# Second attention: where the tensor engine issues a group's first logits, two groups ahead

## The reference, cut to what matters

```python
std_logits = jnp.einsum('bhqd,bhkd->bhqk', q, k) * scale
incidence = jnp.einsum('bqhp,bkhp->bhqk', read_lines, J_write)
weights = decays[:, None, None] ** diffs_pos[None] * past[None].astype(x.dtype)
bias = incidence * weights[None] * bias_scale[None, :, None, None]
logits = jnp.where(causal_mask[None, None], -jnp.inf, std_logits + bias)
attn = jax.nn.softmax(logits, axis=-1)
out = jnp.einsum('bhqk,bhkd->bqhd', attn, v).reshape(B, T, D)
return out @ w_out.T + b_out
```

## Time and profile before

| | us |
|---|---|
| median of 3 runs | 1814.32 |
| lowest, highest | 1808.61, 1819.41 |
| span of the profiled execution, first to last instruction | 1776.1 |
| median of the runs less that span (start and end of the program, not in the profile) | 38.2 |
| busy in the span: tensor, vector, scalar, GpSimd | 1455.7, 1274.7, 935.2, 694.1 |
| mean granted clock of the tensor engine | 0.912 |

### The profile page before, as it was taken

How to read it: one execution, slowest core, us unless ns; L and a number is a source line. 1 busy time by engine, 2 the same in 40 slices (tenths; PEclk the granted TensorE clock), 3 DMA queues, 4 the chain that set the end, 5 groups by cost and what they waited for, 6 DMA issues and landing times. The chain is left out here.

```text
span 1776.1 us, 37567 instructions
## 1 busy us (share of the span) xinstructions
PE 1455.7 (82%) x11726; PEld 964.8 (54%) x11726; DVE 1274.7 (72%) x3482; ACT 935.2 (53%) x1914; POOL 694.1 (39%) x812
## 2 busy tenths in 40 slices
PE   3999999999999729995378887878888887837993
PEld 1224334333343319994256766666666665627993
DVE  6777888888787435555777879697978786834555
ACT  2577777777775505662435455454545453314561
POOL 3122342633520334554233344444444541233552
PEclk8699999999998969997689999898999998978997
DMA  6211111111110332222544443434344434132225
GB/s 158 66 42 59 47 52 53 61 53 49 49 62 15 128 123 67 73 72 82 164 150 126 126 128 106 131 109 129 112 125 122 130 111 138 38 130 56 71 72 162
DMA packets 122418, 166.37 MB, mean 94 GB/s; under 512 B 21490, under 2 KB 96018, under 8 KB 121586
## 3 DMA queue, kind: packets, MB, share of 16 engines
q1 hardware_dynamic: 113330, 145.69, 28.1%
q0 software_dynamic: 8896, 18.30, 3.0%
HBM read 116.04 MB, written 47.60 MB: 92 GB/s over the span
## 5 line engine op out<-in xcount | busy, mean ns | idle before, releaser
L1124 DVE TENSOR_REDUCE a_M<-a_F 128x1 f32<-128x512 f32 x512 | 325.8, 683 | 90.0 <-PE a_F L1318 88.1
L1025 ACT ACTIVATE L_W<-a_ST 128x512 f32<-128x512 f32 x512 | 276.8, 595 | 89.1 <-PE a_ST L1359 88.3
L2028 ACT ACTIVATE L_W<-c_ST 128x1024 f32<-128x1024 f32 x160 | 163.3, 1021 | 188.4 <-PE c_ST L2408 141.1
L2630 ACT ACTIVATE L_hT<-L_P,L_W1s 128x128 f32<-128x128 f32 x600 | 171.5, 368 | 142.9 <-PE L_P L2711 110.6
L2616 POOL DMA_INDIRECT L_yd<-L_ys,L_di x150 | 163.1, 1087 | 151.6 <-DVE L_ys L2662 147.2
L489 POOL DMA_INDIRECT L_xd<-L_XN,L_place_i x128 | 124.4, 972 | 146.5 <-issue 131.9
L1359 PE MATMUL a_ST<-L_W 74*128 74x512 bf16 x512 | 168.9, 395 | 11.1 <-ACT L_W L1025 6.3
L1318 PE MATMUL a_F<-L_W 72*128 72x512 bf16 x512 | 167.1, 403 | 7.7 <-DVE a_M L1124 6.9
L2702 PE MATMUL L_P<-L_xT,L_W1s 128*128 128x128 f32 x1200 | 161.0, 278 | 0.0
L2711 PE MATMUL L_P<-L_W,L_hT 128*128 x1200 | 159.1, 276 | 0.1
L2407 PE MATMUL c_ST<-ident,c_SD 128*128 128x128 f32 x512 | 149.7, 292 | 5.5 <-ACT L_W L2028 5.5
(11 more groups left out here) (430 smaller groups left out, 3164.9 us busy)
## 6 DMA issues: line engine op xcount, KB each, us to landing
c_QS<-c_q SPq DMA_DIRECT2D x32, 504.0 KB
c_QS<-c_rd SPq DMA_DIRECT2D x32, 378.0 KB
L_xg<-L_xd SPq DMA_DIRECT2D x150, 64.5 KB
L_W<-a_q SPq DMA_DIRECT2D x32, 288.0 KB
L_W<-a_k SPq DMA_DIRECT2D x96, 96.0 KB
L_W<-c_k SPq DMA_DIRECT2D x96, 96.0 KB
L_W<-in_L_w SPq DMA_DIRECT2D x8, 1024.0 KB
c_QI<-c_r SPq DMA_DIRECT2D x32, 216.0 KB
```

What stands on the lines that cost most here:

```text
L1025: act.activation(PT[:, j, kk, :], ST[:, kk, :], ACT.Exp).then_inc(sem(exped), 1)
L1124: dve.tensor_reduce(M[:, t, h:h + 1], FB[n % BANKS][:, :], AX_X, ALU.max).then_inc(sem(maxed), 1)
L2028: act.activation(PT[:, j, :, :], ST[:, :, :], ACT.Exp).then_inc(sem(exped), 1)
L2630: act.activation(hT[:, n % 2, f, :], PS[2 + 2 * (n % 2) + f // 2][:, (f % 2) * P:(f % 2 + 1) * P], func, bias=W1s[:, n % WB, F + f:F + f + ...
```

## The change

The tensor engine's order within a group changes, and nothing else. The first logits of the group two ahead leave slot 3 (after the fourth score tile and spot 6), and stand after the last score tile, the first value product and the turned maxima, ahead of the other three value products. Spot 7 so comes right behind spot 6. The last two groups have no such logits.

```diff
                         if j < QUAD - 1 and has_quad(g, 1, n1):
                             b, q = next_quad(i, g)
                             logits(b, QUAD * q + j + 1)
-                        if j == QUAD - 1 and has_quad(g, 2, n1):
-                            b, q = next_quad(i, g, 2)
-                            logits(b, QUAD * q)
                         spot(g, 2 * j + 1)
                     scores(i, g, QUAD)
                     values(i, g, 0, prev)
                     if has_quad(g, 1, n1):
                         turn_max(*next_quad(i, g))
+                    if has_quad(g, 2, n1):
+                        b, q = next_quad(i, g, 2)
+                        logits(b, QUAD * q)
                     for kt in range(1, T):
                         values(i, g, kt, prev)
```

## The result

The changed kernel took 1837.97 us (median of 4, 1830.78 to 1844.22) against 1811.46 us for the kernel before in the same round (median of 4, 1808.59 to 1819.41). The ratio is 1.0107, 95% interval [1.0062, 1.0151]: slower by 1.1%, where 1809 us had been forecast. The miss is 29 us.

A forecast was written before the change was run, and what follows sets the result against it. Neither engine is full; a group's length is its unchanged vector work to the join plus the tail. Gains 14.0 + 4.3 + 4.1 less 7.6 and 9.1 (clock) leave 5.7 us: 1809 us, own range 1802 to 1817, 8 in 10 1794 to 1826.

The forecast's parts named there:

- the gains of groups 1 to 3: Tails, from a group's join to the next reciprocal, shorten by 4.1, 14.0 and 4.3 us as transfer waits go.
- 38.2 us between runs and span: Median of the runs less the profiled span, added to the forecast span of 1770.4 us to give 1808.6.
- Group 0's tail: Join to next reciprocal in group 0: 4.57 us instead of 3.42, a loss of 7.6 us over eight tails.
- The vector engine's new wait: Behind the join the vector engine gets INC late and idles 0.6 to 0.8 us, covered by the tensor engine's path.
- The clock: Longer idling ahead of group 0's join makes the tensor clock fall: 1.3 us each, seven groups, 9.1 us lost.
- six of six: In this loop, the clock fell behind every idle stretch of 1.77 us and more, to 1.2 GHz for about 3.4 us.
- Group 2: Seven tails: transfer waits partly become the second projection's wait for the scalar engine; 76.7 to 62.7 us, a gain of 14.0.
- Group 1: Eight tails go from 44.3 to 40.2 us, a gain of 4.1, with spot 7's routing turn waiting about 0.7 us.
- Group 3: Seven tails go from 38.3 to 34.0 us, a gain of 4.3: the transfer wait goes, six tails become 4.57.
- The rivals: Clock holds (0.27, say 1800 us); clock falls in nearly every group (0.18, 1831); waits only change names (0.15, 1815).
- The slow one: Rival, chance 0.18: the clock falls in nearly every group that the vector engine bounds, on the path; 1831 us.
- My list of signs: Trace signs for or against; wrong if group 0's tail stays near 3.4, pre-join vector work gets gaps, or transfers land later.

The follow-up runs named there:

- moved_g2: The change made only in group 2, the other groups in the order of the kernel before, on a chip without the standstill: 1772.28 us, ratio 0.9939.
- after_5: The changed kernel run again with no further edit, on another chip without the standstill: 1778.73 us, ratio 1.0000 to the kernel before.

## Why the prediction was wrong

**The step that failed** is the gains of groups 1 to 3 (4.1, 14.0 and 4.3 us, 22.4 together), all read from transfer waits of one traced execution. On the chip with the standstill, whose times are like those of the first runs, these waits were mostly not there to be taken away. Measured there: +11.1 us in the three groups, where -22.4 was forecast. That is 33.5 us too low. Group 0 was forecast 3.7 us too high. Together the loop was forecast 29.8 us too low, and the time missed by 29. The warning stood in my table: 38.2 us between runs and span. I took them for start and end of the program, which are 1.6 us. On the chips whose executions look like the trace, the three groups gained 19.1 of the 22.4 us and group 0 lost 18.4 for 16.7: -0.7 us for a forecast of -5.7.

**Group 0's tail** was right: 4.57 forecast, 4.79 measured. The turned maxima start 0.06 us behind the join as worked out; they, the logits and the three value products take 0.10, 0.09 and 0.05 us more than their prices (batch 3). The vector engine's new wait of 0.81 us (forecast 0.6 to 0.8) is covered by the tensor engine's path, as said: the maxima are done some 4.0 us behind the join, and the reciprocal still waits 0.78 us for the tensor engine.

**The clock** was right in kind and near in size. The idle stretch ahead of the join is 2.06 us in batches 2 to 6 (forecast 2.4). A fall costs 1.6 us (6.36 less 4.78) for 1.3. It came in six of group 0's seven in the run without the standstill, 9.6 us for the forecast's 9.1, and in three of seven, in batches 2, 4 and 6, in the two runs of the kernel after with it. With the scatters moved to group 3 it came in five of seven on that same chip, so the chip alone doesn't decide it. The Trainium skill (TensorE: Matmul & The Clock Gate, "What's actually happening") has the slow state as the default that activity must lift. The traces agree in direction, but the same idle stretch isn't always followed by a fall: batch 3's group 0 of the kernel after has a granted clock of 1.00 on both sides of its join. The forecast's "six of six" behind 1.77 us and more didn't hold for the new waits.

**Group 2**, where nothing stalls, gained 16.7 us for 14.0, and the second projection waits for the scalar engine as said (0.78 us). With the standstill it lost 4.8. Its tails in batches 2 to 5 are 10.0 to 10.5 us at low clock, 7.77 without.

**Group 1** gained 2.1 us without the standstill and 0.4 with it, for 4.1. Five of its eight tails became 4.79, batch 0's stayed at 5.8, and batch 1's rose from 4.77 to 7.06. Spot 7's routing turn (L377) waits 1.4 to 2.1 us for the scalar engine there, where I had put 0.7. The forecast's eight tails of group 1 add up to 40.4 us, not 40.2.

**Group 3** was wrong in either case: -0.3 and +6.7 us for -4.3. No transfer waits there after the change, as said; but the tail of 4.79 takes part of that back, and the seven tails gain 2.3 us only. The rest goes in work ahead of the join, which I had called untouched: without the standstill the join's last operation (L2168) takes 0.85 us instead of 0.18 in batches 3 to 5, 2.0 us together. In batch 4 it starts at 1325.49, just behind a product of GpSimd (L1623, 1325.31 to 1327.26); in the first trace GpSimd did nothing at that point. On the stalling chip there was nothing to take back from (five of seven tails were 3.42 already).

**The rivals.** None was what happened. The slow one, at 1831 us, was nearest by its time, but not by its mechanism: the falls behind a join stay in group 0 (and behind the standstill), and groups 1 and 3 hold 4.79. My list of signs had the true one, gaps in the vector work ahead of the join, without a price or a cause.

**What stays open.** Why the engines that wait for the tensor engine are held back beside a row of scatters on one chip and not on the others; whether scatters in pairs avoid it; whether the logits ahead of the turned maxima gain there. From the tails I would expect they do (group 0 and 3 back at 3.4 to 3.9 from 4.79), but that is argued, not shown. Of the 44 us between the two spans of the kernel before, the loop accounts for 14.5, and 29.6 lie ahead of the first reciprocal (935.7 against 965.3). Part of these looks like the same thing: the first layer has eight rows of eight scatters too. At one of them, the last scatter and a wait of the vector engine (L1112), in the second trace of the kernel before and then in the first:

```profile
617.77 0.96 POOL L489 DMA_INDIRECT L_xd<-L_XN,L_place_i  x1 [0.30 <-issue]
620.67 0.69 DVE L1112 TENSOR_TENSOR a_XC<-a_PC,a_XC 128x512 f32<-128x512 f32 x1 [12.67 <-remote]
...
595.26 0.69 DVE L1112 TENSOR_TENSOR a_XC<-a_PC,a_XC 128x512 f32<-128x512 f32 x1 [7.86 <-PE a_PC L1304]
```

That wait is 12.5 to 12.7 us in all five traces with the standstill and 7.86 in the first trace of before, in `moved_g2` and in `after_5`. What the rest of the 29.6 us is stays open.

## What to carry to other kernels

Before a gain is read from waits, hold the traced execution's span against the timed runs: here a gap of 2% meant that the trace was of another state of the machine, and the waits for transfers were not those of the timed runs. Sum waits over the same groups and not over the same microseconds, since a slower run moves its last groups out of the window. A forced idle stretch ahead of a join is the place for work that another step needs later; the same burst put just behind the join cost 1.37 us here in each group that had no late transfer, and left the idle stretch for the clock to fall in. An experiment per group of a pipeline (0 and 3 alone, 2 alone) told in two runs what the whole hid: a loss and a gain that cancelled.

## What the runs showed of the hardware

- In the four traces taken on one chip, and in the changed kernel's first trace, engines that wait for the tensor engine get on 0.8 to 2.6 us behind the end of the eighth of eight scatters in a row. They have waited 4.5 to 8.4 us by then, in five groups of a run. In the eleven traces from three other chips the longest wait of L2147 is 0.7 us and that of L1924 3.7. The scatters' own pace is the same with and without it: 1.26 us apart.
- Its price for the kernel before is hidden in part: the loop is 14.5 us longer, while the five long waits alone are 27.7 us. The tails are 25.1 us shorter, where most of the late transfers were waited for.
- The same idle stretch of 2.06 us at the same place of the loop (group 0, batches 2 to 6 of the kernel after) was followed by a fall of the clock in three of five batches in both traces with the standstill in group 2, and in all five where it lay in group 3 or was absent.
